# Mixture stage of a two-layer transformer step: one list of steps per queue, sorted by places of its own; row maximum and exponentials in halves of eight heads

## The chip, the cores and the metric

The kernel runs on one core of a Trainium2 chip. The metric is the time of one execution on the device, in microseconds (us). The core has a matrix engine (TensorE, "PE" in the rows; its weight loads are "PEld"), a vector engine (VectorE, DVE), a scalar engine (ScalarE, ACT), a general engine (GpSimd, POOL) and SyncE (SP), which issues DMAs. Each engine works through its own instructions strictly in order, and engines wait for one another through semaphores. The matrix engine writes into PSUM, which has 8 banks of 128 partitions x 512 f32.

## The reference, cut to what matters

Four layers follow one another on x of shape (8, 1024, 256). The change touches the stage that computes the second layer (its router has already chosen 128 of 1024 tokens for each of the 8 batches) and the first part of the third:

```python
    x_sel = take(layernorm(x), idx)                # 128 tokens a batch
    h = rmsnorm(x_sel, g1)
    q, k, v = (h @ W_qkv.T)                        # 16 heads of 16
    att = softmax(where(mask, -inf, q k / 4))      # 16 x 128 x 128
    x_attn = (att v) @ W_out.T
    h2 = rmsnorm(x_sel + x_attn, g2)
    x_ff = silu(h2 @ W1.T) * (h2 @ W2.T) @ W3.T
    x = x + layernorm(out.at[idx].set(x_sel + x_attn + x_ff))
    # third layer, first part, on xn = layernorm(x)
    q = xn @ Wq.T + bq                             # all 1024 tokens
    scores_sample = q . k[sample_idx]              # 35 sampled tokens
    m = scores_sample.max(-1)                      # then the top 35 queries of each head
```

## The kernel before, in words

The program has stages in sequence, each a block of its own: attention (`attention_loop`), a setup with the choice of tokens, the mixture stage (`mod_loop`, `mod_all`), `top_queries`, and `prob_loop` with the last layer. Only the mixture stage is changed.

The mixture stage takes the 8 batches one by one through some 45 small steps. A step has a name and a batch, and each engine knows what it has to do in it. In the order in which a batch passes them:

- **pick** (L1195): POOL fetches the 128 chosen rows by an indirect DMA. **l1, xs, hn**: layer norm and first rms norm, statistics and scaling on DVE, the powers on POOL.
- **hnt**: two transposes on PE (L1369), copied to SBUF by ACT (L1490). **k_t, q_t, val** (L1397, L1402): the projections. DVE spreads k into a block-diagonal operand `kbd` (L1279), ACT copies q and the values.
- **s 0, s 1**: scores of eight heads each on PE (L1409); DVE scales, masks and stores them into the single buffer `sm` (L1287). **less**: one reduction over all 16 heads for the row maximum (L1293, DVE). **exp**: 16 activations, one a head (L1516, ACT).
- **pt 0, pt 1**: transposes of the exponentials on PE (L1416), copied by ACT (L1522, half 0) and DVE (L1297, half 1). **o**: 16 products with the values (L1423), divided on DVE (L1302 to L1304). **ot, xa**: transposes and the output projection (L1431), then DVE and POOL for the second rms norm, **hn2**, **hnt2**.
- **gate, up** (L1441), **ff** (L1447): the gated feed-forward part. ACT applies Silu (L1537), DVE multiplies (L1319) and makes **x2**, **xn2**; POOL does the powers and writes both back by indirect DMAs (**put**, L1236 and L1238).
- **load** (L1174): SP loads all 1024 rows of the batch, 1 MB. **samp** (L1244): POOL fetches the 35 sampled rows. **xst, ks**: sampled keys (L1452, L1458). **xt 0/1** (L1376), **q 0/1** (L1470), **qt 0/1** (L1376): all rows transposed, projected, transposed again; ACT copies (L1550, L1556), DVE adds the bias (L1354). **store_q** (L1179): SP stores q, 1 MB. **ms 0 to 7** (L1482): scores against the samples on PE, their maximum on DVE (L1360).

What sets the order: the table `PLACES` gives every step one number, `PERIOD` is 30, and `mod_order` sorts the steps of all batches by 30 x batch + place. **All five queues use this one list**, each leaving out the steps in which it has nothing to do. Places reach from 0 to 88, so the list has about three batches in work at a time.

PSUM is dealt out in the order of the list: steps in `PAIR_STEPS` take the next of 3 slots of two banks, those in `SINGLE_STEPS` the next of 2 slots of one bank. PE may write into a slot when the copy of its last use is done (`pe.wait_ge(taken, uses)`), and an engine that reads waits for `filled`. SBUF buffers are double, triple or fourfold (`xg` 4, `xs` and `xa` 3, most others 2), but `kbd`, `sm`, `cpt`, `cxnt`, `cq` and `qtt` are single.

```python
PERIOD = 30.0
def mod_order():

    placed = [(PERIOD * b + at, (kind[0], b, *kind[1:])) for b in range(B) for kind, at in PLACES.items()]
    return [step for _, step in sorted(placed, key=lambda p: p[0])]
```

In the rows, a matmul of f32 operands shows as two instructions (12 matmuls of gate are a row x24).

Of the kernel before, what the change touches and what calls it, by code (L numbers as in the profile page):

```python
# [664 lines left out]
def attention_all(nc, io, w, ps, mem, e):  # L665
# [413 lines left out]
PERIOD = 30.0  # L1079
PLACES = {  # L1080
    ("pick",): 0, ("l1",): 3, ("xs",): 5.5, ("hn",): 6.5, ("hnt",): 7.5, ("k_t",): 9, ("q_t",): 9.5, ("val",): 10,
# [5 lines left out]
} | {("ms", j): 81 + j for j in range(NT)}  # L1087


def mod_order():  # L1090

    placed = [(PERIOD * b + at, (kind[0], b, *kind[1:])) for b in range(B) for kind, at in PLACES.items()]
    return [step for _, step in sorted(placed, key=lambda p: p[0])]


def mod_loop(nc, io, w, ps):
    with Memory(nc) as m:
# [15 lines left out]
        names = """l1_stat l1_step l1_rstd l1_rms hn_ready less_ready exp_done xa_ss rms_step rms_ready hn2_ready  # L1113
            l2_stat l2_step l2_rstd l3_stat l3_step l3_rstd chosen ksbd_ready q_stored""".split()
        e = {n: m.sem("c_" + n) for n in names}
        for name in ("picked", "x2_put", "xn2_put", "loaded", "sampled"):
            e[name] = [m.sem(f"c_{name}{n}") for n in range(2)]
# [8 lines left out]
def mod_all(nc, io, w, ps, mem, e):  # L1126

    order = mod_order()
    pair_number = {step: k for k, step in enumerate(s for s in order if s[0] in PAIR_STEPS)}
    single_number = {step: k for k, step in enumerate(s for s in order if s[0] in SINGLE_STEPS)}  # L1130
# [34 lines left out]
    with nc.Block() as block:  # L1165
        @block.sync
        def _(sp):
            for step in order:
                kind, b = step[0], step[1]
                if kind == "load":  # L1170
                    sp.wait_ge(e["xn2_put"][b % 2], 16 * (b // 2 + 1))
                    if b >= 2:
                        until_filled(sp, "xt", b - 2, NHALF - 1)
# [12 lines left out]
        def _(g):  # L1186
            for step in order:
# [9 lines left out]
                elif kind == "l1":  # L1197
# [15 lines left out]
                elif kind == "hn2":  # L1213
# [6 lines left out]
                elif kind == "x2":  # L1220
# [6 lines left out]
                elif kind == "xn2":  # L1227
# [20 lines left out]
        def _(v):  # L1248
# [7 lines left out]
            for step in order:  # L1256
# [19 lines left out]
                elif kind == "k_t":  # L1276
                    v.wait_ge(filled, uses + 1)
                    for k in range(KC):
# [12 lines left out]
                elif kind == "less":  # L1291
                    nc.vector.drain()
                    nc.vector.tensor_reduce(smx[:, r, :], sm[:, :, :], AX.X, ALU.max, negate=True)\  # L1293
                        .then_inc(e["less_ready"], 1)
                elif kind == "pt" and a[0] == 1:
                    v.wait_ge(filled, uses + 1)
                    nc.vector.tensor_copy(pt[:, HC:H, :], src.rearrange("p two (h k) -> p (two h) k", k=P))\  # L1297
                        .then_inc(taken, 1)
                elif kind == "o":
                    v.wait_ge(filled, uses + 1)  # L1300
                    of_heads = src[:, 0:H * (D + 1)].rearrange("p (h d) -> p h d", d=D + 1)
# [10 lines left out]
                elif kind == "hn2":  # L1312
                    v.wait_ge(e["rms_ready"], b + 1)
                    nc.vector.scalar_tensor_tensor(hn2[:, r, :], xa[:, b % 3, :], scale[:, 2, r:r + 1], w["g2"][:, :],
# [28 lines left out]
                elif kind == "ks":  # L1343
                    v.wait_ge(filled, uses + 1)
                    for k in range(KC):
# [3 lines left out]
                elif kind == "q":  # L1349
                    n, = a  # L1350
                    v.wait_ge(filled, uses + 1)
                    if b:
                        v.wait_ge(e["q_stored"], 16 * b)
                    nc.vector.tensor_tensor(q[:, 4 * n:4 * n + 4, :],  # L1354
# [10 lines left out]
        def _(pe):  # L1365
# [14 lines left out]
            for step in order:  # L1380
                kind, b, a = step[0], step[1], step[2:]
                if kind not in PAIR_STEPS and kind not in SINGLE_STEPS:
                    continue
# [103 lines left out]
        def _(act):  # L1487
# [4 lines left out]
            for step in order:  # L1492
# [5 lines left out]
                if kind == "hnt":  # L1498
                    act.wait_ge(filled, uses + 1)
                    if b >= 2:  # L1500
                        until_filled(act, "val", b - 2)
                    chunks(hnt[:, r, :, :], src).then_inc(taken, 1)
                elif kind == "q_t":
                    act.wait_ge(filled, uses + 1)
                    if b >= 2:
                        until_filled(act, "s", b - 2, KC - 1)
# [6 lines left out]
                elif kind == "exp":  # L1513
                    act.wait_ge(e["less_ready"], b + 1)
                    for h in range(H):
                        last = nc.scalar.activation(sm[:, h, :], sm[:, h, :], ACT.Exp, bias=smx[:, r, h:h + 1])  # L1516
                    last.then_inc(e["exp_done"], 1)
# [10 lines left out]
                elif kind == "hnt2":  # L1528
                    act.wait_ge(filled, uses + 1)
                    if b >= 2:  # L1530
                        until_filled(act, "up", b - 2)
# [670 lines left out]
```

## Time and profile before

| | us |
|---|---|
| median of 3 runs (lowest, highest) | 3021.38 (3014.14, 3021.91) |
| the profiled execution: its own time | 3020.04 |
| the profiled execution: span from first to last instruction | 3018.3 |
| PE busy in the span | 2563.3 (85%) |
| DVE busy | 1633.8 (54%) |
| ACT busy | 1206.3 (40%) |
| POOL busy | 910.8 (30%) |
| mixture stage: first fetch issued | at 1518.83 |
| mixture stage: first matmul | at 1525.39 |
| mixture stage: last reduction over | at 1998.25 |

The page cuts the span into 40 slices of 75.5 us; the mixture stage is slices 20 to 26. There PE is 5, 8, 8, 8, 8, 9 and 4 to 7 tenths busy, while in the attention stage before it every slice shows nine tenths or more, and the clock that was granted to TensorE falls from 9 tenths or more to between 7 and 9. Busy time of PE counts an instruction's whole duration and so says less than the time from one group's start to the next one's.

### The profile page before, as it was taken

To read this page: it belongs to the slowest core of one execution; us is meant where nothing else is said; L and a number is where in the kernel's file an instruction comes from. 1 tells how busy PE (TensorE), PEld (TensorE's weight loads), DVE (VectorE), ACT (ScalarE), POOL (GpSimd) and SP (SyncE) were. 2 spreads that over 40 slices of the span, in tenths; PEclk is the share of its full clock that TensorE was granted. 3 is DMA by queue.
4 is the path that set the end of the run, shared out by engine and by line. 5 is a ranking of instruction groups with operands and counts; after the bars stand their busy time and mean duration, and the time that the engine had idled before them with its cause. 6 is when DMAs were issued, how large, how long until landed. Compare 5 with 4: busy or idle time off the path is not lost. (4 is left out here: it accounts for less than half of the span.)

```text
span 3018.3 us, 40610 instructions
## 1 busy us (share of the span) xinstructions
PE 2563.3 (85%) x14316; PEld 1528.3 (51%) x14316; DVE 1633.8 (54%) x4637; ACT 1206.3 (40%) x1994; POOL 910.8 (30%) x1442
## 2 busy tenths in 40 slices
PE   3799999999999999995158888947899999999997
PEld 2244444444545444442137777734566666656664
DVE  2667676767677675772743444342444443443443
ACT  1266666666566666564122232202322322322221
POOL 6040524426160716134012111011324233243142
PEclk9699999999999999998577887968999999999999
DMA  2442250605251524301401111121111021021010
GB/s 96 120 127 72 87 154 35 197 32 170 61 179 51 160 81 141 86 17 56 151 4 54 34 50 52 46 56 48 51 35 44 31 69 43 29 71 43 15 43 28
DMA packets 156117, 220.25 MB, mean 73 GB/s; under 512 B 18591, under 2 KB 122987, under 8 KB 149676
## 3 DMA queue, kind: packets, MB, share of 16 engines
q1 hardware_dynamic: 151820, 213.65, 23.0%
q0 software_dynamic: 4096, 4.01, 0.5%
q8 instruction: 115, 1.88, 0.3%
q14 instruction: 86, 0.70, 0.1%
HBM read 113.75 MB, written 103.88 MB: 72 GB/s over the span
## 5 line engine op out<-in xcount | busy, mean ns | idle before, releaser
L1009 ACT ACTIVATE pt<-ps 128x1024 f32<-128x1024 f32 (+3 forms) x768 | 599.8, 811 | 308.3 <-PE ps L924 210.3
L835 DVE CUSTOM_DVE_ANT_0 masked<-ps,mask_q 128x128 bf16<-128x128 f32 (+3 forms) x1024 | 473.4, 485 | 246.1 <-PE ps L902 243.9
L902 PE MATMUL ps<-sk,sq 96*128 96x512 bf16 (+3 forms) x1536 | 427.7, 337 | 66.5 <-DMA sk<-scratch_stacks 28.9
L921 PE MATMUL ps<-sq,sk 99*128 99x512 bf16 (+3 forms) x1536 | 398.7, 329 | 13.6 <-DMA sq<-scratch_nm_parts 11.5
L839 DVE TENSOR_REDUCE mx<-ps 128x1 f32<-128x512 f32 x512 | 351.7, 687 | 91.0 <-PE ps L902 90.5
L940 PE MATMUL ps<-pt,val 128*32 128x512 f32 (+3 forms) x3072 | 328.1, 499 | 3.5 <-ACT yt L1017 3.5
L902 PEld LDWEIGHTS ps<-sk,sq 96*128 96x128 bf16 x1536 | 132.6, 97 | 385.6 <-issue 104.1
L2086 PE MATMUL ps<-w_fc,eyb 128*128 128x256 f32 x1024 | 229.3, 381 | 14.6 <-ACT eyb L2147 7.8
L921 PEld LDWEIGHTS ps<-sq,sk 99*128 99x128 bf16 x1536 | 147.4, 98 | 161.0 <-ACT pt L1009 59.1
L2074 PE MATMUL ps<-eht,w_fc 128*128 128x512 f32 x512 | 223.2, 594 | 1.5 <-ACT eht L2137 1.4
L2086 PEld LDWEIGHTS ps<-w_fc,eyb 128*128 128x128 f32 x1024 | 191.4, 190 | 49.3 <-ACT eyb L2147 16.1
L924 PE MATMUL ps<-w_mask_kq,w_ident 128*128 128x128 bf16 x1024 | 204.1, 220 | 0.0
L1937 DVE TENSOR_TENSOR ehh<-ps,ehh 128x256 f32<-128x256 f32 x64 | 27.2, 425 | 267.1 <-PE ps L2086 155.5
L2147 ACT ACTIVATE eyb<-ps,w_fc_b 128x512 f32<-128x512 f32 x128 | 87.9, 687 | 206.3 <-PE ps L2074 199.4
L781 POOL CAST nmp<-nmr 32x128 bf16<-32x128 f32 x32 | 9.1, 284 | 506.8 <-ACT nmr L1042 506.8
L2074 PEld LDWEIGHTS ps<-eht,w_fc 128*128 128x128 f32 x512 | 96.6, 190 | 118.7 <-issue 114.8
L959 PE MATMUL ps<-xnt,w_wqkv 128*128 128x512 f32 x256 | 118.4, 608 | 0.8 <-ACT xnt L1036 0.8
L924 PEld LDWEIGHTS ps<-w_mask_kq,w_ident 128*128 128x128 bf16 x1024 | 101.1, 99 | 23.6 <-issue 5.2
L2122 ACT ACTIVATE pr<-ps,nb 112x1024 f32<-112x1024 f32 x40 | 44.5, 1113 | 169.5 <-DVE nb L1875 169.5
L940 PEld LDWEIGHTS ps<-pt,val 128*32 128x32 f32 x3072 | 60.6, 108 | 90.5 <-issue 55.8
L554 POOL TENSOR_SCALAR ertmp<-ermv 128x8 f32<-128x8 f32 x8 | 2.0, 247 | 333.4 <-DVE ermv L549 333.4
L2011 PE MATMUL ps<-ekt,qbd 128*112 128x512 f32 x192 | 88.1, 595 | 9.3 <-ACT pr L2122 9.3
(329 smaller groups left out, 4295.6 us busy)
## 6 DMA issues: line engine op xcount, KB each, us to landing
scratch_stacks<-part SPq DMA_DIRECT2D x32, 768.0 KB, 3.7
sq<-scratch_stacks SPq DMA_DIRECT2D x32, 768.0 KB, 8.9
sk<-scratch_stacks SPq DMA_DIRECT2D x32, 768.0 KB, 11.4
scratch_stacks<-part SPq DMA_DIRECT2D x32, 512.0 KB, 4.6
scratch_x<-xr SPq DMA_DIRECT2D x16, 1024.0 KB, 7.7
x<-in_L_attn_x SPq DMA_DIRECT2D x8, 1024.0 KB, 14.4
scratch_stacks<-part SPq DMA_DIRECT2D x32, 256.0 KB, 4.9
xr<-in_L_attn_x SPq DMA_DIRECT2D x8, 1024.0 KB, 6.3
```

The costliest lines, as they stand in the source:

```text
L835: nc.vector.tensor_tensor_reduce(mem["masked"][:, slot, 0:n], ps[:, RING[slot], 0:n], mem["mask_q"][:, BANK - n:BANK], 1.0, -3e38, ALU.add ...
L839: nc.vector.reduce_max(mx[:, hh, i, half:half + 1], ps[:, RING[slot], 0:n], AX.X)\
L902: nc.tensor.matmul(ps[:, bank, 0:n], sq[0:ROWS, h, i * P:(i + 1) * P], sk[0:ROWS, h, half * BANK:half * BANK + n], start=True, stop=True)\
L921: last = nc.tensor.matmul(ps[:, bank, 0:n], sk[0:ROWS_M, h, j * P:(j + 1) * P], sq[0:ROWS_M, h, q0:q0 + n], start=True, stop=not diag)
L924: last = nc.tensor.matmul(ps[:, bank, 0:P], w["ident16"][:, :], w["mask_kq"][:, :], start=False, stop=True)
L940: last = nc.tensor.matmul(ps[32 * hh:32 * hh + 32, 6, c0:c0 + n], val[:, j, s * HS + hh, :], pt[:, t % 3, hh, 0:n], start=(j == 0), stop=( ...
L959: last = nc.tensor.matmul(ps[:, bank, :], w["wqkv"][:, k, col:col + P], xnt[:, k, n * BANK:(n + 1) * BANK], start=(k == 0), stop=(k == KC ...
L1009: nc.scalar.activation(pt[:, u % 3, 2 * pair:2 * pair + 2, 0:n], ps[:, bank:bank + 2, 0:n], ACT.Exp, scale=SCALE).then_inc(e["exp_done"], 1)
L2011: last = nc.tensor.matmul(ps[0:MR, 2 * (mt % 2) + n, :], qbd[:, k, mt * MR:(mt + 1) * MR], kt[:, k, n * BANK:(n + 1) * BANK], start=(k == ...
L2074: last = nc.tensor.matmul(ps[:, 6 + f % 2, :], w["fc1"][:, k, f * P:(f + 1) * P], ht[:, k, n * BANK:(n + 1) * BANK], start=(k == 0), stop= ...
L2086: last = nc.tensor.matmul(ps[:, 6 + j % 2, 0:C], yb[:, f, t * P:(t + 1) * P], w["fc2"][:, f, :], start=(f == 0), stop=(f == F2T - 1))
L2147: nc.scalar.activation(yb[:, f, :], ps[:, 6 + f % 2, :], ACT.Silu, bias=w["fc1_b"][:, f:f + 1]).then_inc(e["y_ready"], 1)
```

## The change

**Places.** `PERIOD` is 20. `PLACES` becomes two tables. A step on PE has a pair of numbers: its place in PE's list, and its place in the list of the four other queues (DVE, ACT, POOL, SP). `mod_order` returns both lists. The slots of PSUM are dealt out by PE's list. Places reach to 128, so more than six batches are in work at a time. POOL's parts of the norms become steps with places of their own (r1, r2, r3, r4).

**Halves.** `less` and `exp` are each two steps of eight heads, with semaphores of their own; pt 0 waits only for exp 0, pt 1 for exp 1.

**Waits.** Since an engine that reads a buffer is no longer known to have passed it when the list reaches a later step, waits are added before buffers are written again. The matmuls, copies, DMAs and buffers are the same ones.

```diff
-PERIOD = 30.0
-PLACES = {
-    ("pick",): 0, ("l1",): 3, ("xs",): 5.5, ("hn",): 6.5, ("hnt",): 7.5, ("k_t",): 9, ("q_t",): 9.5, ("val",): 10,
+PERIOD = 20
+PRODUCTS_AT = {
+    ("hnt",): (16, 12.5), ("q_t",): (20, 24), ("k_t",): (21, 20.5), ("s", 0): (24.5, 26), ("val",): (25, 25.5),
...
+OTHERS_AT = {
+    ("l1",): 0, ("xs",): 1, ("hn",): 2, ("pick",): 7, ("r1",): 8.5, ("less", 0): 26.5, ("less", 1): 29,
...
 def mod_order():
 
-    placed = [(PERIOD * b + at, (kind[0], b, *kind[1:])) for b in range(B) for kind, at in PLACES.items()]
-    return [step for _, step in sorted(placed, key=lambda p: p[0])]
+    def placed(places):
+        steps = [(PERIOD * b + at, (kind[0], b, *kind[1:])) for b in range(B) for kind, at in places.items()]
+        return [step for _, step in sorted(steps)]
+
+    products = placed({kind: at for kind, (at, _) in PRODUCTS_AT.items()})
+    return products, placed(OTHERS_AT | {kind: at for kind, (_, at) in PRODUCTS_AT.items()})
...
                 elif kind == "less":
+                    n, = a
+                    heads = slice(HC * n, HC * (n + 1))
                     nc.vector.drain()
-                    nc.vector.tensor_reduce(smx[:, r, :], sm[:, :, :], AX.X, ALU.max, negate=True)\
-                        .then_inc(e["less_ready"], 1)
+                    if b >= 2:
+                        v.wait_ge(e["exp_done"][n], b - 1)
+                    nc.vector.tensor_reduce(smx[:, r, heads], sm[:, heads, :], AX.X, ALU.max, negate=True)\
+                        .then_inc(e["less_ready"][n], 1)
...
                 elif kind == "exp":
-                    act.wait_ge(e["less_ready"], b + 1)
-                    for h in range(H):
+                    n, = a
+                    act.wait_ge(e["less_ready"][n], b + 1)
+                    for h in range(HC * n, HC * (n + 1)):
                         last = nc.scalar.activation(sm[:, h, :], sm[:, h, :], ACT.Exp, bias=smx[:, r, h:h + 1])
-                    last.then_inc(e["exp_done"], 1)
+                    last.then_inc(e["exp_done"][n], 1)
...
                 elif kind == "pt":
                     n, = a
-                    pe.wait_ge(e["exp_done"], b + 1)
+                    pe.wait_ge(e["exp_done"][n], b + 1)
...
                 elif kind == "k_t":
                     v.wait_ge(filled, uses + 1)
+                    if b:
+                        until_filled(v, "s", b - 1, 0)
+                        until_filled(v, "s", b - 1, 1)
```

Waits of the same kind are added in DVE's pt 1, o, hn2, ks and q, in ACT's hnt, q_t and hnt2, and in SP's load.

On PE, from the last score products of one batch to the next batch's q projections, the list was this (`sm` the exponentials, `cval` the values, `co` the attention output, `cot` its transpose, `hn` either normed input, `sx` the sampled rows, `cxn` the loaded rows):

```order
L1482 MATMUL ps<-ksbd,qtt 128x280 x16
L1416 MATMUL ps<-w_ident,sm 128x128 x16
L1423 MATMUL ps<-cval,cpt 128x17 x16
L1369 MATMUL ps<-w_ident,co 128x128 x2
L1431 MATMUL ps<-w_mod_wout,cot 128x256 x2
L1369 MATMUL ps<-w_ident,hn 128x128 x2
L1452 MATMUL ps<-w_centre,sx 128x35 x2
L1397 MATMUL ps<-hnt,w_mod_wqkv 128x128 x8
L1376 MATMUL ps<-w_ident,cxn 128x128 x8
```

The same engine in the changed kernel, from the same transposes of the exponentials of one batch to the output projection of that batch:

```order
L1442 MATMUL ps<-w_ident,sm 128x128 x16
L1397 MATMUL ps<-w_ident,hn 128x128 x2
L1484 MATMUL ps<-xst,w_ps_wk 128x35 x4
L1496 MATMUL ps<-w_ps_wq,cxnt 128x256 x8
L1423 MATMUL ps<-hnt,w_mod_wqkv 128x128 x8
L1467 MATMUL ps<-hnt,w_mod_w 128x128 x24
L1449 MATMUL ps<-cval,cpt 128x17 x16
L1496 MATMUL ps<-w_ps_wq,cxnt 128x256 x8
L1435 MATMUL ps<-kbd,cqt 128x512 x2
L1428 MATMUL ps<-w_mod_wqkv,hnt 128x256 x2
L1404 MATMUL ps<-w_ident,cq 128x128 x8
L1508 MATMUL ps<-ksbd,qtt 128x280 x2
```

Between the transposes of the exponentials and the products that need them there was nothing, and there are now five groups of other batches; the transposes of the result (`co`, not shown) follow behind four more.

On ACT, around the exponentials, before:

```order
L1537 ACTIVATE gate<-ps 128x768
L1556 COPY qtt<-ps 128x2x512
L1516 ACT_TABLE_LOAD
L1516 ACTIVATE sm<-sm,smx 128x128 x16
L1556 COPY qtt<-ps 128x2x512
L1522 COPY cpt<-ps 128x1024
L1490 COPY cot<-ps 128x256
```

and in the changed kernel:

```order
L1567 ACTIVATE gate<-ps 128x768
L1540 COPY cval<-ps 128x16x16
L1586 COPY qtt<-ps 128x2x512
L1516 COPY cot<-ps 128x256
L1586 COPY qtt<-ps 128x2x512
L1545 ACT_TABLE_LOAD
L1545 ACTIVATE sm<-sm,smx 128x128 x16
L1573 COPY xst<-ps 128x70
L1580 COPY cxnt<-ps 128x2x512
L1516 COPY hnt<-ps 128x256
L1580 COPY cxnt<-ps 128x2x512
```

Both copies of `qtt` now come ahead of the exponentials, where the second one stood behind them, and the exponentials stand ahead of the copies that the next batches' projections need. On SP, loads (`cxn`) and stores (`cq`) alternate as they did.

## Rows read from the trace of the kernel before

**Rows 1.** Busy time by stretch: us, PE, PEld, DVE, ACT, POOL busy (instructions), granted clock, DMA share, GB/s
```profile
1525.40:1998.20 472.80, 389.50 (x2032) 327.62 (x2032) 191.92 (x292) 119.79 (x239) 64.00 (x114) 0.84 0.14 43
1701.00:1756.00 55.00, 46.49 (x254) 39.05 (x254) 24.48 (x38) 15.08 (x30) 8.76 (x16) 0.88 0.15 48
1702.00:1717.00 15.00, 11.77 (x58) 10.01 (x58) 4.16 (x11) 0.96 (x3) 3.82 (x9) 0.58 0.28 82
1720.00:1737.00 17.00, 17.00 (x102) 14.21 (x102) 5.44 (x6) 3.48 (x4) 0.00 (x0) 1.00 0.00 1
```

**Rows 2.** Timeline of one batch's round: start, us, engine, line, idle before and its releaser
```profile
1701.59 4.45 PE L1423 MATMUL ps<-cval,cpt 128*128 128x17 f32 x32 [1.41 <-DVE cpt L1297]
...
1706.97 0.66 PE L1369 MATMUL ps<-w_ident,co 128*128 128x128 f32 x2 [0.94 <-DVE co L1304]
...
1708.19 2.05 PE L1431 MATMUL ps<-w_mod_wout,cot 128*128 128x256 f32 x4 [0.55 <-ACT cot L1490]
...
1711.77 0.66 PE L1369 MATMUL ps<-w_ident,hn 128*128 128x128 f32 x2 [1.53 <-DVE hn L1274]
...
1713.60 3.78 PE L1397 MATMUL ps<-hnt,w_mod_wqkv 128*128 128x128 f32 x16
...
1746.54 4.04 PE L1482 MATMUL ps<-ksbd,qtt 128*128 128x280 f32 x16 [3.18 <-ACT qtt L1556]
...
1756.10 4.35 PE L1423 MATMUL ps<-cval,cpt 128*128 128x17 f32 x32 [1.41 <-DVE cpt L1297]
```

**Rows 3.** Timeline, PE alone, of the dense part of the same round
```profile
1719.33 0.98 PE L1458 MATMUL ps<-xst,w_ps_wk 128*128 128x35 f32 x8
...
1721.27 2.84 PE L1441 MATMUL ps<-hnt,w_mod_w 128*128 128x128 f32 x24
...
1723.95 1.88 PE L1409 MATMUL ps<-kbd,cqt 128*128 128x512 f32 x4
...
1725.67 3.62 PE L1470 MATMUL ps<-w_ps_wq,cxnt 128*128 128x256 f32 x16
...
1729.12 1.88 PE L1409 MATMUL ps<-kbd,cqt 128*128 128x512 f32 x4
```

**Rows 4.** Timeline of the last batch: two neighbouring reductions of ms, and the last one
```profile
1990.91 0.74 DVE L1360 TENSOR_REDUCE w_measure<-ps 128x16 f32<-128x560 f32 x1 [2.19 <-PE ps L1482]
1991.86 0.74 DVE L1360 TENSOR_REDUCE w_measure<-ps 128x16 f32<-128x560 f32 x1 [0.20 <-PE ps L1482]
...
1997.51 0.74 DVE L1360 TENSOR_REDUCE w_measure<-ps 128x16 f32<-128x560 f32 x1 [0.20 <-PE ps L1482]
```

**Rows 5.** Timeline of the first batch: first matmul, end of exponentials, products with the values
```profile
1525.39 0.69 PE L1369 MATMUL ps<-w_ident,hn 128*128 128x128 f32 x2 [9.85 <-DVE hn L1274]
...
1539.31 4.78 ACT L1516 ACTIVATE sm<-sm,smx 128x128 f32<-128x128 f32 x16 [6.70 <-DVE smx L1293]
...
1549.06 5.43 PE L1423 MATMUL ps<-cval,cpt 128*128 128x17 f32 x32 [1.41 <-DVE cpt L1297]
```

**Rows 6.** Timeline, ACT and DVE around one batch's exponentials
```profile
1738.04 1.01 ACT L1556 COPY qtt<-ps 128x1024 f32<-128x1024 f32 x1 [13.09 <-PE ps L1376]
...
1738.49 2.29 DVE L1293 TENSOR_REDUCE smx<-sm 128x16 f32<-128x2048 f32 x1
1739.07 1.28 ACT L1516 ACT_TABLE_LOAD   x1
```

**Rows 7.** DMA issues of the stage: what, queue, count, KB each, median us to landing
```profile
cxn<-scratch_xn SPq DMA_DIRECT2D x8, 1024.0 KB, 5.8
scratch_q<-cq SPq DMA_DIRECT2D x8, 1024.0 KB, 4.4
```

More of the change, by code:

```diff
@@ L1076 @@
 SINGLE_STEPS = ("hnt", "k_t", "q_t", "val", "o", "ot", "xa", "hnt2", "ff", "xst", "ks")
-PERIOD = 30.0
-PLACES = {
-    ("pick",): 0, ("l1",): 3, ("xs",): 5.5, ("hn",): 6.5, ("hnt",): 7.5, ("k_t",): 9, ("q_t",): 9.5, ("val",): 10,
[5 rows of a table removed]
-} | {("ms", j): 81 + j for j in range(NT)}
-def mod_order():
-    placed = [(PERIOD * b + at, (kind[0], b, *kind[1:])) for b in range(B) for kind, at in PLACES.items()]
-    return [step for _, step in sorted(placed, key=lambda p: p[0])]
+PERIOD = 20
+PRODUCTS_AT = {
+    ("hnt",): (16, 12.5), ("q_t",): (20, 24), ("k_t",): (21, 20.5), ("s", 0): (24.5, 26), ("val",): (25, 25.5),
[6 rows of a table added]
+}
+OTHERS_AT = {
+    ("l1",): 0, ("xs",): 1, ("hn",): 2, ("pick",): 7, ("r1",): 8.5, ("less", 0): 26.5, ("less", 1): 29,
+    ("exp", 0): 29.5, ("exp", 1): 29.5, ("hn2",): 55, ("r2",): 60, ("x2",): 75, ("xn2",): 76.5, ("r3",): 83.5,
+    ("r4",): 86.5, ("put",): 88, ("samp",): 90, ("load",): 113.5, ("store_q",): 122.5,
+}
+def mod_order():
+    def placed(places):
[3 more added lines that the diff above has]
+    return products, placed(OTHERS_AT | {kind: at for kind, (_, at) in PRODUCTS_AT.items()})
 def mod_loop(nc, io, w, ps):
@@ L1126, in mod_all @@
 def mod_all(nc, io, w, ps, mem, e):
-    order = mod_order()
-    pair_number = {step: k for k, step in enumerate(s for s in order if s[0] in PAIR_STEPS)}
-    single_number = {step: k for k, step in enumerate(s for s in order if s[0] in SINGLE_STEPS)}
+    products, others = mod_order()
+    pair_number = {step: k for k, step in enumerate(s for s in products if s[0] in PAIR_STEPS)}
+    single_number = {step: k for k, step in enumerate(s for s in products if s[0] in SINGLE_STEPS)}
     (xg, xs, hn, hnt, qt, kbd, val, sm, smx, pt, rs, o, ot, xa, junk, ss, hn2, hnt2, gate, xp, x2s, xn2s, stats, mv, var,
@@ L1167, in _ @@
         def _(sp):
-            for step in order:
+            for step in others:
                 kind, b = step[0], step[1]
@@ L1186, in _ @@
         def _(g):
-            for step in order:
+            for step in others:
                 kind, b = step[0], step[1]
@@ L1212, in _ @@
                         .then_inc(e["l1_rms"], 1)
-                elif kind == "hn2":
+                elif kind == "r2":
                     g.wait_ge(e["xa_ss"], b + 1)
@@ L1255, in _ @@
             nc.vector.memset(val[:, :, :, D:D + 1], 1.0)
-            for step in order:
+            for step in others:
                 kind, b, a = step[0], step[1], step[2:]
@@ L1313, in _ @@
                     v.wait_ge(e["rms_ready"], b + 1)
+                    if b >= 2:
+                        until_filled(v, "hnt2", b - 2)
                     nc.vector.scalar_tensor_tensor(hn2[:, r, :], xa[:, b % 3, :], scale[:, 2, r:r + 1], w["g2"][:, :],
@@ L1344, in _ @@
                     v.wait_ge(filled, uses + 1)
+                    if b >= 2:
+                        until_filled(v, "ms", b - 2, NT - 1)
                     for k in range(KC):
@@ L1378, in turn_tiles @@
                 return last
-            for step in order:
+            for step in products:
                 kind, b, a = step[0], step[1], step[2:]
-                if kind not in PAIR_STEPS and kind not in SINGLE_STEPS:
-                    continue
                 r = b % 2
@@ L1490, in chunks @@
                 return nc.scalar.copy(into, src[:, 0:C].rearrange("p (k t) -> p k t", k=KC))
-            for step in order:
+            for step in others:
                 kind, b, a = step[0], step[1], step[2:]
@@ L1500, in _ @@
                     if b >= 2:
-                        until_filled(act, "val", b - 2)
+                        for reader in ("k_t", "q_t", "val"):
+                            until_filled(act, reader, b - 2)
                     chunks(hnt[:, r, :, :], src).then_inc(taken, 1)
@@ L1530, in _ @@
                     if b >= 2:
+                        until_filled(act, "gate", b - 2)
                         until_filled(act, "up", b - 2)
```

21 lines of the change are left out of this document (14 added, 7 removed), and 11 rows, old and new, of tables (PLACES, PRODUCTS_AT).

## The prediction

> **What bounds the kernel now.** I read the busy times by stretch first, then the timeline of one round, then the rows of the first and last batch. The program's stages follow one another and only the mixture stage is touched, so the question is when its last reduction ends. It ends at 1998.25 [rows 4]; the first matmul starts at 1525.39 [rows 5].
>
> In between PE is busy 389.5 of 472.8 us at a granted clock of 0.84 of full, DVE 191.9, ACT 119.8, POOL 64.0 [rows 1]. So PE is the bound, but not PE at its best: two losses are to be seen.
>
> - *Waits.* Products with the values start at 1701.59 and again at 1756.10: a round takes 54.5 us [rows 2]. In it PE waits at one chain of a single batch: 1.41 for the copy of the exponentials, 0.94 for the divided output, 0.55 for its transpose, 1.53 for the normed input, and 3.18 for `qtt`, whose copy stands behind the exponentials on ACT [rows 2]. In the 55.0 us stretch PE is busy 46.5, so some 8.5 us a round are idle [rows 1].
> - *Clock.* From 1702 to 1717, where these waits lie close together, the granted clock is 0.58, near the lower level of 1.2 GHz; from 1720 to 1737, where PE is busy 17.00 of 17.00 us, it is 1.00, that is 2.4 GHz [rows 1]. The lower level shows in durations: 16 instructions of 128 columns take 3.78 us at L1397, 24 of them take 2.84 us at L1441 [rows 2, 3].
>
> **What a batch costs PE with neither loss.** Durations of neighbours overlap, so I take the time from one group's start to the next one's.
> - 128 columns: 1723.95 - 1721.27 = 2.68 us for 24, or 0.112 each [rows 3]. A batch has 118 (gate and up 48, q_t and k_t 16, pt 16, xt 16, qt 16, hnt, hnt2 and ot 6): 13.2 us.
> - 512 columns: 1.72 for 4 [rows 3]; 8 a batch: 3.4.
> - 256 columns: 1729.12 - 1725.67 = 3.45 for 16, or 0.216 each [rows 3]. q 32, ff 12, val 4, xa 4: 52, or 11.2.
> - ms: one 0.95 us after another [rows 4], 8 times: 7.6.
> - ks and xst: 0.98 for the eight of ks as its own duration, some 0.8 from start to start [rows 3]; 1.1 for both.
> - o: no row shows its 32 loads at the full clock alone. They take 5.43 us in the first batch [rows 5], when the engine had hardly worked, and 4.35 and 4.45 later, in stretches of mixed clock [rows 2]. Half of 5.43 is 2.7, the lower bound; 4.4 is the upper. I take 2.8, near the lower, because the neighbours will then be dense.
>
> Sum: 13.2 + 3.4 + 11.2 + 7.6 + 1.1 + 2.8 = **39.3 us a batch**, against a round of 54.5. Eight batches: 314.
>
> **The change part by part.**
>
> *The order on PE.* I followed the new lists through one round of the middle, with PE's groups laid end to end by the durations above, and asked at each group when its input and its PSUM slot are ready. The five waits of rows 2 all lie behind work of other batches now: o has ks, a q half, both projections, gate and up ahead of it (13 us, for copies of 1.0 to 1.2); ot has a q half, s, val, qt and ms; xa has s, ms, ff and qt; hnt2 has six ms, xt, hnt and pt. The second qt copy comes ahead of the exponentials: it lands about 1.2 us after its transposes, and the first ms that needs it starts 5 us after them. I find no wait longer than the cover. The thinnest covers are 0.8 us (pt 1 for the slot of xt 0, which ACT copies after the exponentials) and 1.5 to 2 us (s 1 and ms 6 for their slots).
>
> *The halves.* On DVE one reduction of 2.29 us becomes two of some 1.2 us [rows 6]: a tenth or two of a microsecond more on an engine that is under half busy [rows 1], so I cost it at nothing. On ACT the same 16 activations take 4.78 us [rows 5]. They now start behind the second qt copy (1.01) and a table load (1.28) [rows 6], and end 1.0 + 1.3 + 4.8 = 7.1 us after qt's transposes. PE reaches pt 0 of that batch about 9 us after them (xa 0.9, six ms 5.7, xst 0.3, xt 1.8, hnt 0.2), and pt 0 needs only the first half, 2.4 us sooner; pt 1 has 2.5 us to spare. Table loads stay at two a batch. If this cover goes, PE waits at pt once a batch, and next late is the k projection behind it.
>
> *Added waits.* Each asks for something that PE did a batch or two ago in the middle of the stage; I cost them at nothing, and the walk above is their cover. On POOL, r1 of a batch stands behind the put of an older one; xs needs r1 only 4 us after l1, which covers its five small operations.
>
> *SP.* Load of batch b stands behind the store of batch b - 1, as before, but that store is now late: the store follows q 1's bias, and PE reaches xt of the next batch about 16 us later. A load alone lands in 5.8 us, a store in 4.4 [rows 7]; one after the other, 10.2. That is covered in the middle, and by 0.7 us for batch 6. For batch 7 the distance is only some 8 us, so PE waits 0 to 2 us; I take 1.
>
> *The start.* Batch 0 is alone as before: exponentials over at 1544.1, its o over at 1554.5 [rows 5]. In the new list the first transposes may start when half the exponentials are done, but o needs both halves, and in the gap PE does batch 1's hnt and projections. So o still ends at 1554.5 with 2.0 us of batch 1 done. From there to the first xst PE has 45.8 us of work at the full clock (attention and feed-forward of batches 0 and 1, attention of 2, half of 3, 58.7 in all, less 12.9 done). To this I add 5 us of waits, since the exponentials of batches 1 and 2 are not yet covered, and 7.5 us for some 15 us at the lower clock. First xst at 1613; bounds 1603 (waits of 3 us alone) and 1625 (all 45.8 at a clock of 0.8).
>
> *The sum.* From the first xst all is PE's work: 314.4 - 58.7 = 255.7. End: 1613 + 255.7 + 1.0 (last reduction) + 1 (load of batch 7) + 5 for small bubbles (under 1 us a round, my choice; the dense stretch of rows 1 shows none) = 1876. Against 1998.25 the stage is **122 us shorter**, and what follows starts earlier by as much. The profiled execution took 3020.0 us, so 2898; the median of the runs shown lies 1.3 above it, so **2900 us**.
>
> *A rule against this.* The rows say that PE keeps 2.4 GHz where it works without a gap [rows 1]. The Trainium skill ("TensorE: Matmul & The Clock Gate", section "A second HAM failure mode: psum-queue depth-cycling") tells of a kernel that cycled through PSUM banks and paused so briefly and often between groups that its clock went back and forth all the time. This kernel turns its slots over 31 times a batch. By the rule the clock would stay mixed, which is the second case below; rows 1 speak against it, because the turn-over is as quick from 1720 to 1737, and the clock is 1.00 there.
>
> **The rivals.**
> - *A, 0.74: PE back to back, full clock.* 2900, with 2880 to 2925 from the bounds of o, of the start and of bubbles.
> - *B, 0.10: the waits go, the clock stays mixed.* PE then needs the busy time that it has now, 389.5, and some 20 us idle at the start and end: 1525.4 + 389.5 + 20 = 1935, or 63 saved: 2957.
> - *C, 0.10: an in-order wait that I missed.* ACT and DVE each have a list in which a copy that PE needs stands behind one that waits for PE; pt 1 has the thinnest cover. 4 us a round over 7 rounds is 28: 2928.
> - *D, 0.03: slower, by the load behind the store.* It decides when store and load together take over 16 us, and costs each batch the excess. To be slower than before it must cost 122/7 = 17 us a batch, so a landing at 33 us. 10.2 us [rows 7] speaks against it, as does a DMA share of 0.14 in the stage [rows 1]. At 35 us the excess is 19 us over 7 rounds, 133 in all: 3033.
> - *E, 0.03: no change.* The single buffers `kbd`, `sm` and `cpt` and their new waits hold the batches to the old round, whatever the list says: 3020. Against it: each is written and read again within half a round in the walk.
>
> **The numbers.** This kernel can be told from no change at 0.3%, 9 us. A, B and C are faster: 0.94; E 0.03; D 0.03. The range leaves out B's far end, D and E: 2880 (A's lower bounds) to 2950 (beyond C, most of the way to B).
>
> **What would show it.** Right: a round of 39 to 41 us between products with the values, granted clock of 0.97 or more from 1615 on, idle time before L1449, the transposes of `co` and of the second `hn`, and the first ms after qt 1 near zero; first xst near 1613; stage over near 1876. Wrong: PE idle behind "ACT sm" at pt or "DMA cxn" at xt every round (C, D); a clock under 0.9 in a stretch where PE is over 95% busy (B); or a round over 50 us (E).

## The result, and the profile after

| | before | after |
|---|---|---|
| median (lowest, highest) of 4 runs each, us | 3018.18 (3014.14, 3021.91) | 2902.62 (2898.68, 2904.42) |
| ratio of the two, 95% interval | | 0.9616 [0.9597, 0.9634] |
| profiled execution, us (its span) | 3020.04 (3018.3) | 2904.42 (2902.7) |
| last reduction of the stage over | 1998.25 | 1880.00 |

The change saves 3.8%, 115.6 us; 2900 was forecast. The stage ends 118.25 us earlier. The 2.6 us between the two were lost behind the stage, in code that the change does not touch, and were not looked into.

The page of the changed kernel, its first lines and two rows of the 40 slices (72.6 us each; the stage is now slices 21 to 25):

```profile
span 2902.7 us, 40662 instructions
PE 2517.6 (87%) x14316; PEld 1496.0 (52%) x14316; DVE 1636.3 (56%) x4645; ACT 1203.3 (41%) x1992; POOL 910.6 (31%) x1442
PE   3699999999999999999218999957899999999997
PEclk9699999999999999999658999978999999999998
```

Matmuls, and the other engines' busy times, are what they were; PE's fell by 46 us because it ran at the lower clock for less time. The stage in stretches, after, with the columns of [rows 1]: us, busy time of PE, PEld, DVE, ACT, POOL, granted clock, DMA share, GB/s.

```profile
1525.40:1880.00 354.60, 343.15 (x2032) 295.07 (x2032) 194.06 (x300) 116.24 (x237) 63.86 (x114) 0.95 0.19 58
1525.40:1560.00 34.60, 26.33 (x124) 19.64 (x124) 19.91 (x26) 11.50 (x35) 5.55 (x12) 0.84 0.03 8
1560.00:1607.00 47.00, 44.60 (x278) 38.25 (x279) 27.12 (x41) 20.54 (x48) 12.36 (x23) 0.89 0.12 35
1607.00:1645.00 38.00, 38.00 (x246) 33.41 (x245) 23.17 (x41) 15.15 (x32) 10.11 (x19) 1.00 0.22 67
1645.00:1685.00 40.00, 40.00 (x247) 34.71 (x246) 22.54 (x36) 12.98 (x24) 7.42 (x13) 0.96 0.21 64
1685.00:1725.00 40.00, 40.00 (x236) 34.51 (x235) 21.58 (x31) 12.42 (x28) 7.56 (x14) 0.91 0.21 64
```

The same 2032 instructions that took 472.8 us [rows 1] take 354.6. PE stood idle for 83.3 us of the stage before and for 11.5 now, so 72 of the 118 us are waits that are gone; the other 46 are busy time, shorter because less of it runs at the lower clock. From 1607 on PE is busy in every microsecond shown. The two rows to keep in mind are the last: 40.00 of 40.00 us busy, and the clock still only 0.96 and 0.91.

PE's waits from the first matmul to the end of the stage, after (engine and line, what it waited for: us in total, times, longest):

```profile
PE ps L1397 <- DVE hn L1286: 9.9, 1, 9.9
PE ps L1442 <- ACT sm L1545: 7.6, 5, 2.1
PE ps L1435 <- DVE kbd L1294: 2.5, 1, 2.5
PE ps L1617 <- PEq L93: 1.7, 1, 1.7
PE ps L1423 <- ACT hnt L1516: 0.5, 1, 0.5
```

The first row is the wait ahead of the stage's first matmul, which stood there before too [rows 5]; L1617 lies behind the stage. The other three belong to the start, all before 1587. The five waits that a round had [rows 2] are gone.

### The profile page after: what moved, and what is told of

It is laid out like the page before. It is cut to its first block and busy times, and to the rows that moved or that the text cites. A ratio compares the mean times of both kernels' runs of the same rounds, so it can differ in the third digit from the quotient of the medians.

```text
span 2902.7 us, 40662 instructions
## 1 busy us (share of the span) xinstructions
PE 2517.6 (87%) x14316; PEld 1496.0 (52%) x14316; DVE 1636.3 (56%) x4645; ACT 1203.3 (41%) x1992; POOL 910.6 (31%) x1442
## 5 line engine op out<-in xcount | busy, mean ns | idle before, releaser
L767 POOL CAST part<-qk 128x512 bf16<-128x512 f32 x64 | 39.0, 609 | 184.6 <-ACT qk L1048 184.6
```

## The experiments

Each kernel's ratio is to the kernel before, timed beside it, whose own median lies between 3018.2 and 3020.4 us. Edits are of the changed kernel, except where "before" is in the name. In the profiles the stage's first matmul comes between 1521.6 and 1526.6, though the code ahead of it is the same; so where two kernels are compared in the start, what counts is the time from that matmul on.

### What lowers the clock while PE is never idle

The timeline of PE, after, where the clock was 0.91 (start, us, engine, line):

```profile
1662.63 3.64 PE L1449 MATMUL ps<-cval,cpt 128*128 128x17 f32 x32
...
1704.75 4.36 PE L1449 MATMUL ps<-cval,cpt 128*128 128x17 f32 x32
1708.95 6.34 PE L1496 MATMUL ps<-w_ps_wq,cxnt 128*128 128x256 f32 x16
1715.13 1.88 PE L1435 MATMUL ps<-kbd,cqt 128*128 128x512 f32 x4
```

and two stretches of it:

```profile
1704.75:1708.50 3.75, 3.75 (x32) 3.75 (x31) 0.96 (x1) 0.00 (x0) 0.00 (x0) 0.86 0.02 4
1708.95:1713.60 4.65, 4.65 (x12) 3.75 (x13) 0.68 (x2) 0.00 (x0) 0.00 (x0) 0.50 0.00 0
```

The clock falls to 1.2 GHz within the products with the values, with no gap anywhere near: the q half behind them takes 6.34 us where it took 3.62 [rows 3]. These are the narrowest products of the round, 17 columns each. I had not expected this, so three kernels change these products alone.

**x1_wide_values.** Each product writes up to seven heads' columns, of which later ones overwrite all but the first head's; the result is the same.

```diff
 for h in range(H):
-    last = nc.tensor.matmul(into[:, h * (D + 1):(h + 1) * (D + 1)], pt[:, h, :], val[:, r, h, :],
+    upto = min(H, h + 7)
+    last = nc.tensor.matmul(into[:, h * (D + 1):upto * (D + 1)], pt[:, h, :], val[:, r, h:upto, :],
                             start=True, stop=True)
```

> The changed kernel with one edit: each of the 16 products with the values writes up to seven heads' columns (119) in place of one head's 17; each later product overwrites all but its own 17, so the result is the same. In the changed kernel's trace the group takes 3.64 us for 32 instructions (0.114 each, the same as for 128 columns), so the columns should cost nothing. Theory (the narrow group is what lets TensorE's clock fall in the middle of gapless work): no stretch at 1.2 GHz between first xst and the end, the round 42 to 44 us falls to 40 to 40.5, the stage is 8 to 10 us shorter: 2893. Rival (the falls have another cause, such as the long gapless stretch or DMA traffic): the clock still falls near the q half after o, 2902. If the wide products cost time after all: the group takes over 4 us and the kernel is slower.

Measured: 2892.22 us, ratio 0.9568 [0.9551, 0.9585]. Its group of products, and one stretch:

```profile
1702.70 3.64 PE L1450 MATMUL ps<-cval,cpt 128*128 128x119 f32 x32
```

```profile
1690.00:1730.00 40.00, 40.00 (x252) 34.81 (x251) 24.19 (x38) 14.66 (x30) 7.84 (x16) 1.00 0.20 64
```

Seven times the columns cost nothing (3.64 us either way) and the falls are gone. In the whole stretch from the first sampled keys to the last matmuls PE is busy in every microsecond, at a clock of 1.00:

```profile
1607.68:1870.50 262.82, 262.82 (x1627) 230.36 (x1626) 145.31 (x231) 83.27 (x153) 45.93 (x79) 1.00 0.22 70
```

From one batch's sampled keys to the next one's it is 40.43, 40.43 and 40.44 us (batches 1 to 4), where the changed kernel has 42.1, 43.8 and 42.1.

**x2_double_values.** The 16 products are issued twice.

```diff
-for h in range(H):
+for h in (*range(H), *range(H)):
```

> The changed kernel with the 16 products with the values issued twice (same result). Theory (narrow group lowers the clock, PE's own work sets the time): the group takes 7.3 us, so 3.6 x 8 = 29 us more work, and now the clock falls in every round inside it or behind it, some 3 us x 8 on top, of which about 9 are there already: 2902 + 29 + 15 = 2946. Rival (falls have another cause): 2902 + 29 = 2931 and the falls come no oftener. If PE were not the bound in the stage, under 2920.

Measured: 2955.15 us, 0.9786 [0.9766, 0.9806]. One group and its stretch:

```profile
1737.99 11.33 PE L1449 MATMUL ps<-cval,cpt 128*128 128x17 f32 x64
```

```profile
1730.00:1770.00 40.00, 40.00 (x217) 35.24 (x216) 17.27 (x26) 8.07 (x14) 5.35 (x11) 0.83 0.20 61
```

At 2.4 GHz the 64 would take 2 x 3.64 = 7.3 us. They take 11.3 here, the longest of the eight groups; the others take 8.5 to 10.8, so every group loses some. The clock is 0.83 in a stretch that PE fills. The kernel is 52.5 us slower than the changed one, 29 for the extra work and 23.5 on top. The theory had 15 on top: the direction is right, the size 9 us too low.

**x3_interleaved_values.** The 16 narrow products go two and two between the matmuls of the q half behind them; not one product is added or widened.

```diff
+for out, left, right in (held[1][2 * (KC * t + k):][:2] if held else []):
+    value = nc.tensor.matmul(out, left, right, start=True, stop=True)
```

> The changed kernel with the products with the values spread two and two between the matmuls of the q half that follows them (batches 0 to 2 of the list that have no such neighbour keep theirs in one group). Theory (a narrow group in one piece lowers the clock): no fall, 8 to 10 us shorter, 2893, and perhaps less, if the loads of the narrow products go beside the wide ones. Rival: only the amount of work counts, 2902.

Measured: 2893.93 us, 0.958 [0.9563, 0.9597], clock 1.00 from 1610 to the stage's end at 1870.6 and rounds of 40.43. So it is the run of narrow products without anything wider between them that loses the clock, not their number in the round.

### Where the halves pay

**x4_whole_maximum.** The new lists, with the maximum and the exponentials of all 16 heads as one step each again.

```diff
-    ("l1",): 0, ("xs",): 1, ("hn",): 2, ("pick",): 7, ("r1",): 8.5, ("less", 0): 26.5, ("less", 1): 29,
-    ("exp", 0): 29.5, ("exp", 1): 29.5, ("hn2",): 55, ("r2",): 60, ("x2",): 75, ("xn2",): 76.5, ("r3",): 83.5,
+    ("l1",): 0, ("xs",): 1, ("hn",): 2, ("pick",): 7, ("r1",): 8.5, ("less", 0): 29,
+    ("exp", 0): 29.5, ("hn2",): 55, ("r2",): 60, ("x2",): 75, ("xn2",): 76.5, ("r3",): 83.5,
...
-                    heads = slice(HC * n, HC * (n + 1))
+                    heads = slice(0, H)
...
-                    pe.wait_ge(e["exp_done"][n], b + 1)
+                    pe.wait_ge(e["exp_done"][0], b + 1)
...
-                    for h in range(HC * n, HC * (n + 1)):
+                    for h in range(H):
```

> The changed kernel with row maximum and exponentials undivided, both transposes of the exponentials waiting for all 16 heads; lists as in the change. Theory (the halves matter only where nothing else covers, that is in the start with batches 0 to 2; from the first xst on all 16 exponentials end before PE reaches the transposes): 3 us a batch in the start, 6 to 10 in all: 2910. Rival (the halves carry a good part of the gain, 2.4 us a round): 8 x 2.4 = 19 or more: 2921.

Measured: 2922.0 us, 0.9681 [0.9662, 0.97]. The time is the rival's, though the place is the theory's. Its transposes of the exponentials:

```profile
1547.81 3.41 PE L1442 MATMUL ps<-w_ident,sm 128*128 128x128 f32 x16 [8.29 <-ACT sm L1545]
...
1569.70 3.65 PE L1442 MATMUL ps<-w_ident,sm 128*128 128x128 f32 x16 [7.52 <-ACT sm L1545]
...
1599.82 3.65 PE L1442 MATMUL ps<-w_ident,sm 128*128 128x128 f32 x16 [4.14 <-ACT sm L1545]
...
1630.23 2.00 PE L1442 MATMUL ps<-w_ident,sm 128*128 128x128 f32 x16 [1.84 <-ACT sm L1545]
```

Four waits of 21.8 us in sum, where the changed kernel has five of 7.6, and then none: the first sampled keys come at 1625.64 instead of 1608.05, and from there to the end of the stage it is 272.35 us, against 271.95. So the halves are worth 17.6 us in the start and little in the rest: the difference there is 0.4, and of the four waits only the last, 1.84, lies behind the first sampled keys. Both kernels lose some 7 to 8 us there to the clock, which blurs a difference of this size.

**y3_before_halves.** The kernel before, with the halves alone (places 17, 17.5 and 19, 19.5).

> The kernel before with only the halves of the change: maximum and exponentials of eight heads each, list and places as before. In the middle PE waits 3.18 us a round for the qtt copy that stands behind the exponentials; these start some 1.1 us sooner, behind the first half of the maximum. Theory (halves matter where exponentials are waited for): 1 us a round and 3 to 5 in the start, 3008 to 3012. Rival (the halves carry much of the gain by themselves): under 2990.

Measured: 3015.53 us, 0.9982 [0.9972, 0.9993], some 5 us, and less than expected. The `qtt` copy still stands behind the exponentials in ACT's list, and PE waits 2.7 us for it where it waited 3.18 [rows 2]. Halves without an order that lets something through between them bring little.

### One list or two

The change has two lists, one for PE and one that DVE, ACT, POOL and SP share.

**y4_one_list.** All queues sorted by PE's places.

```diff
-    return products, placed(OTHERS_AT | {kind: at for kind, (_, at) in PRODUCTS_AT.items()})
+    return products, placed(OTHERS_AT | {kind: at for kind, (at, _) in PRODUCTS_AT.items()})
```

> The changed kernel with PE's places for all queues: DVE, ACT, POOL and SP take each step that PE also has in PE's order. All else is the change (halves, more batches in work). Theory (the gain is PE's order and the covers in it, which are thick): up to 8 us slower than the change, at most 2911. Rival (lists of their own carry a large part, because a copy in PE's order stands behind one that isn't ready): over 2930, with PE idle in every round.

Measured: 2913.8 us, 0.9641 [0.9623, 0.9659]: 11 us above the changed kernel, 3 above what the theory allowed and 16 under the rival. PE's waits of the stage up to 1700, and a stretch of the middle:

```profile
PE ps L1442 <- ACT sm L1545: 12.2, 5, 4.4
PE ps L1435 <- DVE kbd L1294: 2.5, 1, 2.5
PE ps L1442 <- ACT cxnt L1580: 2.5, 1, 2.5
```

```profile
1690.00:1730.00 40.00, 39.83 (x251) 34.38 (x250) 23.30 (x38) 14.57 (x30) 8.34 (x15) 1.00 0.18 57
```

From its first matmul to its first sampled keys y4 takes 94.0 us where the changed kernel takes 82.6, with a wait of 2.51 us for a copy of loaded rows behind that. Thereafter a round takes 40.7 to 40.9 us. That is less than the changed kernel's 42.1 to 43.8, because the clock falls of the changed kernel are not there (1.00 from 1660 to 1800), and 0.45 more than x1's 40.43, which has none either. So the 11 us are net of some luck with the clock: from first matmul to last reduction the stage takes 367.3 us in y4, 354.6 in the changed kernel and 344.7 in x1. What places of their own bring to the four other queues thus lies between 13 and 23 us, a tenth to a fifth of the gain; PE's new order, with more batches in work, brings the rest. How this rest divides between order and number of batches was not tried.

### How thin the covers are

**z2_exponentials_late.** The exponentials are moved by 4.5 places in ACT's list, behind the copies of the next batches' transposes.

```diff
-    ("exp", 0): 29.5, ("exp", 1): 29.5, ("hn2",): 55, ("r2",): 60, ("x2",): 75, ("xn2",): 76.5, ("r3",): 83.5,
+    ("exp", 0): 34, ("exp", 1): 34, ("hn2",): 55, ("r2",): 60, ("x2",): 75, ("xn2",): 76.5, ("r3",): 83.5,
```

> The changed kernel with the exponentials placed later in the list of ACT, DVE, POOL and SP: behind the copies of xst, xt 0, hnt and xt 1 of the round, in place of ahead of them. Nothing else differs. Theory (the prediction's walk): the last of these copies ends 4.0 us after the round's first xst, table load and eight exponentials 3.7, so pt 0 starts at 7.7 in place of 2.4 and pt 1 waits another 1.5: 5 to 7 us a round, and idle PE that brings the clock down too; over some 6 rounds of the middle 35 to 50 us, PE idle before the transposes of the exponentials on ACT: 2935 to 2955. Rival (covers are thicker than walked, or waits shift without loss): under 2920.

Measured: 2946.56 us, 0.9758 [0.9744, 0.9773]. In its timeline:

```profile
1724.13 1.94 PE L1442 MATMUL ps<-w_ident,sm 128*128 128x128 f32 x8 [5.22 <-ACT sm L1545]
...
1726.47 1.94 PE L1442 MATMUL ps<-w_ident,sm 128*128 128x128 f32 x8 [0.40 <-ACT sm L1545]
```

This is the mechanism of the prediction's rival C: two steps of ACT in other places, and 44 us of the 116 are gone. The first wait is the one that the walk through the lists gave (7.7 - 2.4 = 5.3 us, measured 5.22 in most rounds); the second was put at 1.5 and is 0.40. In sum PE waits 40.6 us for the exponentials, 33 more than in the changed kernel, and in stretches of 50 us from 1650 to 1850 the clock is 0.86 to 0.93. So such a wait can be told from the lists and the durations before anything runs.

### Waits and clock in the kernel before

The prediction put the low clock of 1702 to 1717 [rows 1] down to the waits there. After x1 the narrow products are a second suspect.

**y1_before_wide_values.** The kernel before with x1's edit.

> The kernel before with the one edit that took the changed kernel's clock falls away: products with the values of up to 119 columns, same result, same time for the group (0.114 us an instruction). In the kernel before the clock is at 1.2 GHz from about 1704.6 to 1718 in a round, and it falls in the middle of this group. Theory of the prediction (the waits around the group let the clock fall): no change, 3020. Theory after the first four runs (the narrow group lets it fall): the 13 us stretch runs at 2.4 GHz and the round loses 5 to 6 of its 54.4 us, 7 times 6 and the start: 2975. Both together: some rounds only, between the two.

**y2_before_filled_waits.** The kernel before with transposes of the identity, whose output nobody reads, ahead of four steps in which PE waits.

```diff
+FILLERS = {"o": 4, "ot": 2, "xa": 1, "hnt": 4}
...
+                if kind in FILLERS and b:
+                    for _ in range(FILLERS[kind]):
+                        nc.tensor.transpose(into[:, 0:P], w["ident"][:, :], w["ident"][:, :])
```

> The kernel before with transposes of the identity put into the PSUM slot that comes next, ahead of PE's waits in o (4), ot (2), xa (1) and hnt (4), from batch 1 on; what they write is overwritten. They keep PE at work in waits of 1.41, 0.94, 0.55 and 1.53 us and should end before these do (0.9, 0.45, 0.2 and 0.9 us at 2.4 GHz; about twice that at 1.2 GHz, when hnt's would overrun by 0.3). Theory of the prediction (the waits let the clock fall): 2.4 GHz throughout, 5 to 6 us a round, 2975. Theory of the narrow group: the clock falls as before, 3020 or up to 3 us slower.

**z1_before_wide_and_filled.** The kernel before with both.

> The kernel before with both edits that did nothing alone: the wide products with the values, and the transposes of the identity in PE's waits. Alone, each leaves about as long a stretch at 1.2 GHz as there was: with the wide products it begins at 1710.8, behind the waits, in place of 1704.6; with the filled waits it begins inside the narrow group again. Theory (two causes, either of which is enough): with both gone PE runs the stretch from o to the k and q projections at 2.4 GHz, 4 to 6 us a round; the wait of 3.18 us for qtt is not filled and may still bring a fall in ms. 7 rounds: 2980 to 2995. Rival (in the kernel before a chain across engines sets the round, and PE's clock is not on it): 3013 as with the filled waits alone.

| | us | ratio to before |
|---|---|---|
| y1, wide products | 3018.61 | 0.9988 [0.9978, 0.9998] |
| y2, filled waits | 3013.83 | 0.9973 [0.9962, 0.9984] |
| z1, both | 3007.06 | 0.9957 [0.9943, 0.997] |

Neither comes near the 2975 that was expected of a repaired clock: each time the other theory's figure, about 3020, is the nearer one. In y1 the fall starts later, among the waits. Its stretches:

```profile
1706.00:1710.00 4.00, 2.17 (x13) 1.44 (x11) 1.91 (x6) 0.37 (x1) 1.53 (x5) 1.00 0.63 219
1710.00:1712.00 2.00, 0.66 (x2) 0.29 (x2) 0.95 (x4) 0.11 (x1) 1.56 (x4) 0.57 0.03 11
1712.00:1720.00 8.00, 6.60 (x29) 6.55 (x30) 2.75 (x3) 0.96 (x4) 0.50 (x1) 0.50 0.02 5
```

In y2 it starts in the narrow products in this round, as in the kernel before:

```profile
1694.00:1698.00 4.00, 4.00 (x28) 3.40 (x27) 3.11 (x6) 1.01 (x1) 1.85 (x2) 1.00 0.14 36
1698.00:1702.00 4.00, 3.03 (x26) 3.00 (x26) 0.88 (x1) 0.00 (x0) 1.25 (x2) 0.95 0.34 100
1702.00:1708.00 6.00, 5.41 (x20) 4.13 (x21) 1.80 (x6) 0.37 (x1) 2.21 (x6) 0.50 0.44 152
```

So in y1 the waits lower the clock without a narrow group. The other way round y2 shows less, because its transposes fill the waits only in part: 0.97 us ahead of the products, 0.34, 0.25 and 0.64 behind them are left in this round. That narrow products can do it without any wait is shown by the changed kernel. With both edits z1 has a clock of 0.94 in a round's stretch, and yet the round is 53 to 56 us:

```profile
1640.00:1700.00 60.00, 51.13 (x304) 43.28 (x303) 25.42 (x41) 15.55 (x31) 9.16 (x18) 0.94 0.21 63
```

PE now comes sooner to one of its waits and stands there longer, and behind this wait the clock still falls for a while. The two largest waits of z1's rounds, the same two in one round, and the stretch behind the first:

```profile
PE ps L1461 <- DMA sx<-scratch_xn,w_samp: 19.5, 8, 10.1
PE ps L1491 <- ACT qtt L1565: 19.1, 6, 3.2
```

```profile
1704.27 0.60 PE L1461 MATMUL ps<-w_centre,sx 35*128 35x35 f32 x4 [1.88 <-DMA sx<-scratch_xn,w_samp]
...
1737.44 4.04 PE L1491 MATMUL ps<-ksbd,qtt 128*128 128x280 f32 x16 [3.18 <-ACT qtt L1565]
```

```profile
1704.00:1708.00 4.00, 3.73 (x19) 3.72 (x20) 1.14 (x1) 0.22 (x1) 0.00 (x0) 0.61 0.00 0
```

The wait for the sampled rows, 0.3 us or less in a usual round of the kernel before (10.3 us in sum over 3 waits, of which 9.8 one), is 0.5 to 1.9 us a round here, 19.5 over 8. The wait for `qtt` is as long as it was. This is the rival's mechanism, and my expectation for z1 was some 12 to 27 us too low. From 1525.4 to 1985 the clock rose from 0.83 to 0.91 and the kernel gained 13 us. What the clock would bring at 1.00 throughout, in the old order, no run shows; what it did bring came back in part as waits.

### The best version

**z3_wide_filled_start.** The changed kernel with x1's wide products, and with transposes of the identity in PE's waits of the first three batches.

```diff
+FILLERS = {("s", 0, 0): 5, ("pt", 0, 0): 4, ("pt", 0, 1): 4, ("pt", 1, 0): 5, ("pt", 1, 1): 7, ("pt", 2, 0): 3}
```

> The changed kernel with the wide products and, in the start alone (batches 0 to 2), transposes of the identity in PE's waits ahead of s 0 and of the transposes of the exponentials. From the first xst on the wide kernel runs at 2.4 GHz with PE busy all the time, so only the start is left: 81 us for 58.7 us of work, with 15 us idle and a clock of 0.87. Theory: some 2 to 5 us, 2888 to 2890. Rival (the start is bound by batch 0's chain through DVE and ACT, which no clock changes): 2892.

Measured: 2885.69 us, 0.9558 [0.9545, 0.9571], 17 us under the changed kernel's median. Under x1's it is 6.5, but the two ratios, 0.9558 and 0.9568, have intervals that overlap. The start from the first matmul to the first sampled keys, of x1 and then of z3:

```profile
1526.60:1607.68 81.08, 70.47 (x406) 57.42 (x406) 47.90 (x69) 32.87 (x85) 17.89 (x35) 0.88 0.08 24
```

```profile
1521.60:1598.00 76.40, 69.05 (x434) 56.48 (x435) 47.96 (x69) 32.90 (x85) 17.85 (x35) 0.95 0.08 25
```

Work that nobody needs, put where PE would stand anyway, raises the clock of the start from 0.88 to 0.95, and the start is 4.7 us shorter. (That z3's first sampled keys come 9.7 us sooner than x1's is for the larger half because its stage began 5.0 us sooner.) Of the 4.7 us, 1.35 are lost again at the end, where PE waits for the load of batch 7:

```profile
1841.24 1.94 PE L1405 MATMUL ps<-w_ident,cxn 128*128 128x128 f32 x16 [1.35 <-DMA cxn<-scratch_xn]
```

The stage as a whole takes 341.3 us instead of 344.7. These 3.4 us lie within the 2 to 5 that were expected.

## Why the prediction was right

The time and the stage's end came as put down, and so did the mechanism of case A as far as the waits go; the full clock came only in part. By the steps of the prediction:

- **The five waits of a round vanish: right.** PE's last wait inside the stage is before 1587. (The transposes of the result stand behind five groups in a usual round, as the walk has it, not four.) No copy, store or load took their place, though a load now lands in 7.9 us and a store in 5.3, against 5.8 and 4.4 [rows 7]. The wait of 1 us for the last load did not come, and comes as 1.35 in z3. The thinnest covers (0.8 us at pt 1) held, and z2 shows what a cover that is too thin would have cost.

```profile
cxn<-scratch_xn SPq DMA_DIRECT2D x8, 1024.0 KB, 7.9
scratch_q<-cq SPq DMA_DIRECT2D x8, 1024.0 KB, 5.3
```

- **39.3 us a batch: 1.1 too low.** In x1's dense rounds it is 40.43. The term that was mis-sized is o: 3.49 us from start to start for its 32 instructions at 2.4 GHz, not 2.8. That is 0.109 each, as for the 16 transposes of pt (1.75), and 119 columns take the same. I had halved the 5.43 of the first batch [rows 5]; but that row, like the 4.35 and 4.45, was a mixture of both clocks. Of the remaining 0.4, 0.3 is xst and ks (1.37 us, not 1.1) and 0.2 the groups of 256 columns; the others are within 0.1.
- **First sampled keys at 1613: it was 1608.05.** Of the 5 us, 2.6 are gone at "o still ends at 1554.5": the first batch's o begins at 1548.27, 0.8 sooner than before, and is over at 1551.9, since it takes 3.64 us and not 5.43. The waits behind it are 3.7 us, not 5, and work and lower clock together took 52.4 us, not 45.8 + 7.5 = 53.3. The prediction let the halves free the first transposes, but gave them no price of their own; they are worth 17.6 us (x4), where x4's expectation had 6 to 10. The bound of 1625 does not follow from its reason: all 45.8 us at a clock of 0.8, with 5 us of waits, end at 1617.
- **255.7 us of work behind it, + 1 + 1 + 5: 262.7, measured 272.0.** x1, with the clock at 1.00, needs 1871.28 - 1607.68 = 263.6, and PE has no wait in it. So 8.4 us are the clock's. And the 5 us for bubbles and the 1 for the load of batch 7 were not used for either: there were no bubbles, but the work was 6.9 us longer than the sum had it, 3.5 for o (5 batches at 0.69), 2.2 for xst and ks (8 at 0.27), and the rest mostly the groups of 256 columns.
- **Clock 0.97 or more from 1615 on, a round of 39 to 41 us: wrong in most rounds.** The clock was 1.00, 0.96 and 0.91 in the three stretches from 1607 to 1725 shown above, and from one group of products with the values to the next it was 38.5, 42.1 and 43.8 us. The step that failed is the opening reading that PE keeps 2.4 GHz where it works without a gap. That was read from 1720 to 1737 [rows 1], a stretch in which no narrow products lie.
- **Case B: not what happened, though a piece of it did.** The sign given for B was a clock under 0.9 with PE over 95% busy. Whole rounds stay above it (0.91), shorter stretches do not (0.86 from 1662 to 1674, shown below). The mechanism is another one: PSUM slots turn over as often in x1, where the clock is 1.00, as in the changed kernel. By the rule of the Trainium skill ("TensorE: Matmul & The Clock Gate", section "A second HAM failure mode: psum-queue depth-cycling"), quick turns of the banks with short pauses would have kept the clock mixed; the pauses are gone here (262.82 of 262.82 us busy in x1), so nothing speaks against that rule, and nothing in these runs needs it.
- **Low clock before, put down to the waits: half right.** The waits suffice (y1), but so does a run of narrow products without a wait (the changed kernel). The change took away the first of the two.

In sum, the stage ended 4 us later than 1876 because two errors partly cancel: 5 us too many in the start, and 9 too few behind it, of which 8.4 are a mechanism that the prediction did not have. The size of the waits' part was worked out; that the whole came out within 3 us of 2900 is in part luck.

## What to carry to other kernels

- A stage that PE bounds is costed from start-to-start times, group by group, laid end to end; then each wait of the new list is walked with what stands ahead of it on its own engine. That gave the stage's gain here within 4 us of 118, with the luck told above, and the longer of z2's two waits to a tenth of a microsecond.
- Repairing half of the clock's loss without the order (0.83 to 0.91) brought little, 13 us, where the whole change brought 116: a wait grew where the clock gave. Order first, then the clock.
- The filling of a software pipeline is where splitting a step in halves pays; in the middle it changed 2 us at most.

## What the hardware showed that was not expected

- **A run of narrow products loses the clock without any pause.** 32 instructions of 17 columns at a busy share of 100% are followed by about 5 us at a granted clock of 0.50, in some rounds; doubled, the clock of a whole stretch is 0.83. Widened to 119 columns, or put two and two between wider ones, they leave it at 1.00. This is worth 10 us of 2903.
- **Not in every round.** The fall came with the products at 1704.75, and a shorter one behind those at 1662.63, but none behind those at 1624.09. These are the clocks there, of the changed kernel; y4, with the same narrow products, shows 1.00 from 1690 to 1730. What decides between them stays open.

```profile
1624.00:1634.00 10.00, 10.00 (x62) 8.48 (x61) 3.83 (x5) 0.10 (x1) 0.00 (x0) 1.00 0.05 17
1662.00:1674.00 12.00, 12.00 (x65) 9.97 (x64) 3.60 (x5) 0.00 (x0) 0.00 (x0) 0.86 0.03 8
```

- **Columns up to 119 are free** behind a load of 128 x 128 in f32: the group of 32 instructions takes 3.49 us from start to start with 17 and with 119 columns, 0.109 an instruction, and 128 columns take 0.109 to 0.112.
